# Graph attention with residual and layer norm on one Trainium2 core: the first gram of batch 0 moved into the prologue, and sixteen transposes of the identity at the start

## The reference, cut to what matters

```python
z_l = h @ W_lang.T;  z_g = h @ W_grav.T;  v = h @ W_V.T
zn  = z_l / max(norm(z_l), EPS)
A_l = max(zn @ zn.T, 0) * not_eye
d2  = max(sq + sq.T - 2 * z_g @ z_g.T, 0)        # sq = row sums of z_g * z_g
A_g = exp(-d2 / (2 * sigma**2)) * not_eye
K_l = row_stochastic(A_l * adj);  K_g = row_stochastic(A_g * adj)
K   = w_l * K_l + (1 - w_l) * K_g
out = layernorm(h + (K @ v) @ W_O.T)
```

## Time and profile before

| what | value |
|---|---|
| time, three runs | 970.19, 970.68, 974.04 us (median 970.68) |
| profiled execution: time | 975.67 us |
| profiled execution: span of its instructions | 973.9 us |
| TensorE busy | 959.0 us |
| VectorE, ScalarE, GpSimd busy | 699.9, 322.2, 147.4 us |
| mean granted clock of TensorE | 0.995 |

### The profile page before, as it was taken

How to read it: one execution, slowest core, us unless ns; L and a number is a source line. 1 busy time by engine, 2 the same in 40 slices (tenths; PEclk the granted TensorE clock), 3 DMA queues, 4 the chain that set the end, 5 groups by cost and what they waited for, 6 DMA issues and landing times.

```text
span 973.9 us, 13226 instructions
## 1 busy us (share of the span) xinstructions
PE 959.0 (98%) x4802; PEld 829.3 (85%) x4802; DVE 699.9 (72%) x1954; ACT 322.2 (33%) x632; POOL 147.4 (15%) x155
## 2 busy tenths in 40 slices
PE   9999999999999999999999999999999999999997
PEld 7788888988888888888888889888888888889885
DVE  4557868777786676867777687677857777686588
ACT  4324233232432324233232432324233232432341
POOL 0302011121200212002121200212002121200231
PEclk9999999999999999999999999999999999999999
DMA  8313353432534425354342634424344442623001
GB/s 216 87 34 86 105 128 125 119 128 94 136 98 109 147 87 124 108 123 138 104 123 99 152 98 108 156 88 124 105 116 137 112 127 96 143 93 124 1 23 65
DMA packets 215872, 106.78 MB, mean 110 GB/s; under 512 B 140544, under 2 KB 187648, under 8 KB 215808
## 3 DMA queue, kind: packets, MB, share of 16 engines
q1 hardware_dynamic: 213696, 104.90, 38.6%
q10 hardware_dynamic: 2112, 1.05, 0.4%
HBM read 63.44 MB, written 42.47 MB: 109 GB/s over the span
## 4 chain that ended last, share of the span: by engine, by line
PE 84%; DVE 8%; DMA 3%; SPq 2%; POOL 1%; issue 1%; ACT 1%; POOLq 0%; DVEq 0%
PE ring L326 20%; PE ring L328 20%; PE ring L327 20%; PE g_bank L326 7%; PE g_bank L328 7%; PE g_bank L327 7%; DMA off_turned<-off 1%; SPq L284 1%; DMA off<-off_turned 1%; DVE al L912 1%; DVE bn L950 1%; DVE al L889 1%; DVE kT_lo L745 1%; POOL mask_r L1156 1%; DVE ag L919 1%
## 5 line engine op out<-in xcount | busy, mean ns | idle before, releaser
L731 DVE TENSOR_TENSOR zg_lo<-ring,zg_hi 128x512 fp32r<-128x512 f32 x64 | 43.9, 689 | 106.1 <-ACT zg_hi L568 106.0
L1163 POOL TENSOR_TENSOR rstd<-var_eps,neg_half 128x1 f32<-128x1 f32 x64 | 41.5, 649 | 426.2 <-DVE var_eps L958 426.2
L326 PE MATMUL ring<-xT_hi,wgT_hi 128*128 128x512 f32 x256 | 101.8, 398 | 0.1
L326 PE MATMUL ring<-xT_hi,wlT_hi 128*128 128x512 f32 x256 | 101.1, 395 | 0.0
L327 PE MATMUL ring<-xT_lo,wgT_hi 128*128 128x512 f32 x256 | 100.1, 391 | 0.0
L328 PE MATMUL ring<-xT_hi,wgT_lo 128*128 128x512 f32 x256 | 99.8, 390 | 0.0
L327 PE MATMUL ring<-xT_lo,wlT_hi 128*128 128x512 f32 x256 | 99.7, 389 | 0.0
L328 PE MATMUL ring<-xT_hi,wlT_lo 128*128 128x512 f32 x256 | 99.7, 389 | 0.0
L326 PE MATMUL ring<-wvo_hi,xT_hi 128*128 128x512 f32 x256 | 99.7, 389 | 0.0
L328 PE MATMUL ring<-wvo_hi,xT_lo 128*128 128x512 f32 x256 | 99.6, 389 | 0.0
L327 PE MATMUL ring<-wvo_lo,xT_hi 128*128 128x512 f32 x256 | 99.6, 389 | 0.0
(11 more groups left out here) (126 smaller groups left out, 2214.1 us busy)
## 6 DMA issues: line engine op xcount, KB each, us to landing
xb<-in_x_dram SPq DMA_DIRECT2D x60, 256.0 KB, 4.6
out_dram<-y SPq DMA_DIRECT2D x60, 256.0 KB, 2.0
k_turned<-ag SPq DMA_DIRECT2D x56, 256.0 KB, 2.1
al<-k_turned SPq DMA_DIRECT2D x224, 64.0 KB, 2.0
y<-in_x_dram SPq DMA_DIRECT2D x14, 1024.0 KB, 5.5
off_turned<-off SPq DMA_DIRECT2D x28, 384.0 KB, 2.3
off<-off_turned SPq DMA_DIRECT2D x112, 96.0 KB, 2.2
y<-in_x_dram SPq DMA_DIRECT2D x4, 256.0 KB, 5.7
```

The source lines that it names most:

```text
L326: nc.tensor.matmul(psum, lh, rh, start=k == 0, stop=False)
L731: nc.vector.tensor_tensor(pair[1][:, i, :], bank[:, :], pair[0][:, i, :].bitcast(F32), ALU.subtract).then_inc(evacuated, 1)
L1163: nc.gpsimd.tensor_tensor(rstd[:, i:i + 1], var_eps[:, i:i + 1], neg_half[:, 0:1], ALU.pow)\
```

## The change

The gram of `zg` of batch 0 leaves the head of `batch` and is issued in the prologue, between `zl` 2 and `wvo` 0, behind a wait for the split of `zg`. The batches after the first keep their order. The number of transposes of the identity at the start goes from ten to sixteen. Nothing changes on the other engines.

```diff
-WARM_UP = 10
+WARM_UP = 16
...
                 bank = ring[n % RING]
+                if (kind, i) == ("wvo", 0):
+                    pe.wait_ge(evacuated, PROLOGUE.index(("zg", T - 1)) + 1)
+                    for row_tile in range(T):
+                        gram_row(zg, row_tile, gg_rows)
                 claim_bank(n)
...
             def batch(b, parity, stream):
                 s = Steps(b, stream)
 
-                s.gram_g(0)
+                if b:
+                    s.gram_g(0)
                 s.project("zg", 0)
```

## The result

The changed kernel takes 975.96 us (median of 5, 974.88 to 979.51) against 972.53 (median of 5, 970.19 to 974.04): a ratio of 1.0046, with a 95% interval from 1.0029 to 1.0063. The forecast was 1.0041. The profiled execution took 979.51, the slowest of the five, with a span of 977.8.

The account below looks back on a forecast made before the run. TensorE, busy 959.0 of 973.9 us, was taken as the bound. Terms -3.85 + 5.73 + 1.71 + 0.40 = +3.99 us on 975.67 gave 979.66, factor 1.0041, or 974.6 on the median; range 971.8 to 977.6.

Parts of the forecast that it names:

- The gram fills the prologue's hole, without a hole or a slow stretch behind it.: Prologue, between `zl` 2 and `wvo` 0: the gram runs 30.61 to 37.66, gaining 3.85 us (2.14 hole, 1.71 clock).
- `xT` is bare.: Before batch 1's `zg` 0: the input split after `u` 3, formerly hidden by the gram, leaves a 5.73 us hole.
- The clock falls in the new hole.: After the hole before batch 1's `zg` 0: slower clock costs 1.71 us, bounds none to 3.4.
- The six transposes cost 0.4.: Kernel start: six more identity transposes delay the first product by 0.4 us, bounds -0.46 to +0.5.
- No wait at the second gram.: Batch 0's second gram: with the clock loss TensorE arrives at 77.92, after the 77.39 that `exponent` 0 allows.
- SP's write and four reads and ScalarE's copies take what they took: DRAM path behind batch 0's diagonals: durations unchanged, so `exponent` 0 ends at 77.24, before 74.04.
- nothing else is on SP's queue there: SP's queue at batch 0's write and four reads: claimed free of other work; no separate size.
- The sum.: Whole kernel: -3.85 + 5.73 + 1.71 + 0.40 = +3.99 us, factor 1.0041; chance 0.58.
- rival (a): Prologue hole costs no clock in some executions, so gain 2.14, not 3.85; sum +5.7, factor 1.0058, 976.4 us; chance 0.25.
- need not recur: Profile before: its 3.8 us of waits may be absent elsewhere; that execution is 0.5% above the median shown.
- the 1.71: Prologue, from `wvo` 0 to batch 0's gram: 1.71 us lost to the slower clock, which the change removes.

Follow-up runs that it names:

- early diagonals: Changed kernel with VectorE's diagonals of batch 0 moved in front of its drain of `u` 0; ratio to the kernel before 1.0038, or 1.0026 with 24 matmuls in the new hole.
- the move alone: Changed kernel with ten transposes of the identity instead of sixteen, the gram still moved; ratio to the kernel before 1.0051.
- one-row: Kernel before with only row 0 of batch 0's gram moved into the prologue, the rest left in place, ten transposes; ratio 0.9990.
- two-row: Kernel before with rows 0 and 1 of batch 0's gram moved into the prologue, the rest left in place, ten transposes; ratio 1.0029.
- filled: Changed kernel with idle work in the hole before batch 1's `zg` 0: 46 transposes (ratio to the kernel before 1.0064) or 24 matmuls (1.0060).
- with sixteen: Kernel before with sixteen transposes of the identity instead of ten, the gram in its old place; ratio 1.0001.
- with none: Kernel before with no transposes of the identity at the start instead of ten; 975.83 us in one execution.
- with forty: Kernel before with forty transposes of the identity at the start instead of ten; 975.94 us in one execution.
- the first four experiments: Apparently the sections on the change's two halves, one or two gram rows moved, the new hole filled, and VectorE's diagonals taken early; ratios 0.9990 to 1.0064.
- `zl` 3 first: Kernel before with `zl` 3 put in front of `wvo` 0, `u` 0 waiting step by step, gram in its old place, ten transposes; ratio 0.9974.

## Why the prediction was right

- **The gram fills the prologue's hole, without a hole or a slow stretch behind it.** Shown: 31.01 to 38.06, then nine products at 1.00.
- **`xT` is bare.** Shown by the trace (hole of 5.72, forecast 5.73) and by the kernels that leave more or less of the gram behind.
- **The clock falls in the new hole.** Forecast 1.71 of loss; in `zg` 0 it was 1.41 (4.17 - 2.76) after, and 1.77 with early diagonals. The two later waits that this term was compared with are these, the first followed by the slow stretch of the earlier trace rows, the second by none:

```profile
308.47 0.45 PE L326 MATMUL g_bank<-zl_hi 128*128 128x384 f32 x1 [2.08 <-DVE ag L834]
...
718.02 0.44 PE L326 MATMUL g_bank<-zl_hi 128*128 128x384 f32 x1 [1.34 <-DVE ag L834]
```

- **The six transposes cost 0.4.** First product at 8.16 against 7.78, a difference of 0.38; 0.47 between the means above. That the one pair came so close is in part luck, as the starts inside a group lie up to 1.0 apart, and the times can't tell the cost from nothing.
- **No wait at the second gram.** Wrong by 0.67 in this execution. The step that failed is "SP's write and four reads and ScalarE's copies take what they took": the copies began 1.36 later than that. The sum had 0.5 us to spare there, 77.92 against 77.39, and with reads of the usual length that was enough: the move alone has no wait. The one-row, two-row and filled kernels, where TensorE comes sooner, wait in spite of such reads. The sentence "nothing else is on SP's queue there" overlooks the loads of batch 2's `x` right behind the reads.
- **The sum.** Forecast +3.99 in the trace; the second gram came 4.54 later. The difference, 0.55, is 0.83 of wait and restart (6.41 against 5.58 from the end of `zg` 0 on) less 0.30 of clock, and 0.02 before `zg` 0. That the ratio came out within 0.0005 of the forecast is in part luck: its interval also holds the 1.0058 of rival (a). And the prediction's remark that the 3.8 us of waits in the profile before "need not recur" isn't borne out: waits in front of the second gram add up to 1.5 to 5.0 us in every trace here.
- **Rival (a), that executions of the kernel before need not lose the 1.71, holds for some of them.** All four traces with the hole lost it: from `wvo` 0 to the gram 26.19 us before, 26.19 with sixteen, 26.17 with none, 26.20 with forty. But a loss of 1.71 is 0.0018 of 974 us, so an execution with it shows a mean granted clock of 0.998 at most, and of the 34 executions of the kernel before that stood beside the first four experiments seven show 0.999 or 1.000; their mean is 0.9975. With `zl` 3 first it is 0.9984 over 11 runs: a difference of 0.9 us, half of what the one profile gives. So the loss that the change removes is probably worth less than 1.71 on average, which would be a reason for a ratio a little above the forecast. How often an execution loses it was not measured.

## What to carry to other kernels

Before a block of work is moved into a hole, look at what it hid where it stood: here 7.05 us of gram covered a chain of 5.6 us that began only when the product in front of it ended, and that chain was in no list of waits of the kernel before. Fill a hole with work that covers nothing else, or move only as much as the hole holds, and follow the chain past the first wait: the next one may have half a microsecond to spare. Neither a clock loss nor the length of a transfer read from one profile is that of every execution. The mean granted clock of the timed runs shows whether others had the loss too, though it also counts the clock of idle stretches.

## What the runs showed of the hardware that I had not expected

A hole of 2.0 us in front of `wvo` 0 was followed by a slow stretch in all four traces that have it, while a hole of 2.7 in the two-row kernel's profile left the granted clock at 1.00. Transposes of the identity alone brought the quick rate at the start (477 to 272 ns within forty) and kept it over a hole of 5.7 us (`zg` 0 in 2.90 us instead of 4.17), while in one trace ten of them and sixteen transposes of data, with two short waits between, had not brought it by 8.38 us. In the bare hole itself the granted clock was 0.96 in one profile and 0.70 in another of the same move. The same four reads through DRAM took 3.47 to 3.80 us from issue to ScalarE's copy in nine profiles, 4.31 in one and 4.96 in another, with nothing else of the kernel's ahead of them on SP's queue.
